# Writing out the loops over 208 gather groups in a four-layer graph network on one core

## The reference, cut to what matters

```
x = layernorm(x + attention_layer(x, src, dst, attr))        # stage e0
x = layernorm(x + sparse_mean_layer(x, src, dst))            # stage e1
x = layernorm(x + relational_layer(x, src, dst, edge_type))  # stages e2f and e2b
x = layernorm(x + transformer_layer(x, src, dst))            # two layers inside: e3a and e3b

# the common core of a stage
message = table[row_of_edge]                  # 103125 rows
out = segment_sum(weight * message, dst, num_segments=3125)
```

## Time and profile before

| | us |
|---|---|
| median of 3 runs | 9417.85 (9392.93 to 9419.25) |
| profiled execution, its own time | 9402.77 |
| its span, first to last instruction | 9401.0 |
| PE busy | 5084.4 (54%) |
| POOL busy | 5197.8 (55%) |
| DVE busy | 4670.5 (50%) |
| ACT busy | 1393.1 (15%) |
| mean granted TensorE clock | 0.719 of full speed |

### The profile page before, as it was taken

How to read it: one execution, slowest core, us unless ns; L and a number is a source line. 1 busy time by engine, 2 the same in 40 slices (tenths; PEclk the granted TensorE clock), 3 DMA queues, 4 the chain that set the end, 5 groups by cost and what they waited for, 6 DMA issues and landing times. The chain is left out here.

```text
span 9401.0 us, 104712 instructions
## 1 busy us (share of the span) xinstructions
PE 5084.4 (54%) x17609; PEld 3455.4 (37%) x17610; DVE 4670.5 (50%) x11390; ACT 1393.1 (15%) x5321; POOL 5197.8 (55%) x5325
## 2 busy tenths in 40 slices
PE   3444444455554139667766555555555555555555
PEld 2322222222222014344443333334444454555554
DVE  5565557555563214444444333335555555555555
ACT  3544442000000000000000000002111112111112
POOL 4555551555566740466665666664555554555553
PEclk7777767666666569888887666667777777777777
DMA  2222221222223014444444333332222222222222
GB/s 80 43 43 44 42 43 29 79 78 78 80 81 75 3 33 165 142 127 128 129 128 116 88 88 88 87 87 75 76 76 75 76 78 71 78 78 78 79 79 67
DMA packets 499181, 749.04 MB, mean 80 GB/s; under 512 B 217905, under 2 KB 351398, under 8 KB 498854
## 3 DMA queue, kind: packets, MB, share of 16 engines
q0 software_dynamic: 236352, 604.00, 23.3%
q1 hardware_dynamic: 262758, 144.28, 5.1%
HBM read 623.08 MB, written 124.79 MB: 80 GB/s over the span
## 5 line engine op out<-in xcount | busy, mean ns | idle before, releaser
L291 DVE TENSOR_TENSOR acc<-acc,ps 128x257 f32 (+3 forms) x4992 | 1883.2, 377 | 2418.8 <-issue 1127.2
L303 PE MATMUL ps<-rows,onehot 128*128 128x257 f32 (+1 forms) x4992 | 1879.5, 516 | 1646.3 <-DVE onehot L272 770.2
L263 POOL DMA_INDIRECT rows<-table,gidx x1664 | 1616.4, 971 | 1258.5 <-issue 510.8
L303 PEld LDWEIGHTS ps<-rows,onehot 128*128 128x128 f32 x4992 | 1113.4, 247 | 2471.8 <-issue 1404.6
L303 PE MATMUL ps<-msg,onehot 128*128 128x136 f32 (+1 forms) x4992 | 1295.2, 422 | 837.9 <-ACT msg L712 349.4
L303 PEld LDWEIGHTS ps<-msg,onehot 128*128 128x128 f32 x4992 | 1026.8, 266 | 1079.4 <-issue 890.9
L263 POOL DMA_INDIRECT rows<-table2f,gidx x832 | 796.9, 958 | 875.4 <-DMA table2f<-big 391.9
L263 POOL DMA_INDIRECT rows<-table3a,gidx x832 | 825.8, 993 | 616.6 <-ACT gidx L1202 343.8
L263 POOL DMA_INDIRECT rows<-table3b,gidx x832 | 823.0, 989 | 585.5 <-ACT gidx L1202 286.6
L263 POOL DMA_INDIRECT rows<-table2b,gidx x832 | 796.6, 958 | 473.6 <-issue 246.9
L1243 PE MATMUL ps<-big,msg 128*128 x3328 | 638.9, 353 | 511.8 <-issue 292.3
(11 more groups left out here) (309 smaller groups left out, 4601.1 us busy)
## 6 DMA issues: line engine op xcount, KB each, us to landing
table2f<-big SPq DMA_DIRECT2D x80, 640.0 KB, 4.6
table2b<-msg SPq DMA_DIRECT2D x200, 256.0 KB
rows<-table,gidx POOLq DMA_INDIRECT x1664
slots_d<-recs_d SPq DMA_DIRECT2D x832, 2.5 KB
rows<-table2f,gidx POOLq DMA_INDIRECT x832
rows<-table2b,gidx POOLq DMA_INDIRECT x832
rows<-table3a,gidx POOLq DMA_INDIRECT x832
rows<-table3b,gidx POOLq DMA_INDIRECT x832
```

What stands on the lines that cost most here:

```text
L263: nc.gpsimd.indirect_dma_start(out=rows[:, j, 0:width], out_offset=None, in_=table[:, :], in_offset=bass.IndirectOffsetOnAxis(ap=gidx[:, h ...
L291: nc.vector.tensor_tensor(acc[:, bass.ds(b * width, width)], acc[:, bass.ds(b * width, width)], ps[:, bank + k, 0:width], ALU.add).then_in ...
L303: nc.tensor.matmul(ps[:, bank + k, 0:width], onehot[:, h, k, :], rhs, start=True, stop=True).then_inc(sem(of(s, "tile_sum")), 1)
```

## The change

All loops over the groups become Python loops, so that each group has its own instructions on every engine and n is a number when the program is written. No transfer, no product, no vector operation and no order on an engine is changed. The block numbers remain data: DVE still loads them and works out the address from them, and so does PE for the queries. The loops over the blocks of the dense layers (`blocks`, `dense_act`), over the pairs of relations and over the 25 blocks in SP's `pb_store` stay as they are. A copy of e0, which the program skips if the exponents' range was right, is written out too.

```diff
         def groups(eng, body):
 
-            for n in range(R):
+            for n in range(NG):
                 body(n, n % R)
-            with eng.Fori(R, NG - 2 * R + 1, R) as n0:
-                for h in range(R):
-                    body(n0 + h, h)
-            for n in range(NG - R, NG):
-                body(n, n % R)
...
         def groups_beside(eng, body, unit):
 
             assert NG == PAIRS * (NB + 1)
-            for n in range(PAIRS):
-                body(n, n % R)
-            for j in range(PAIRS):
-                body(PAIRS + j, j % R)
-                unit(0, j)
-            with eng.Fori(2, NB + 1) as i:
+            for i in range(NB + 1):
                 for j in range(PAIRS):
                     body(i * PAIRS + j, j % R)
-                    unit(i - 1, j)
+                    if i > 0:
+                        unit(i - 1, j)
...
@@ att_groups
-            with eng.Fori(R, NG - 2 * R + 1, R) as n0:
+            for n0 in range(R, NG - R, R):
                 for h in range(R):
                     step(n0 + h, h, NG)
...
@@ e1 on DVE, the groups with the sort
-                with dve.Fori(0, SORT_IT) as i:
+                for i in range(SORT_IT):
...
@@ e1 on DVE, the last groups
-                with dve.Fori(rest, NG // R) as i:
+                for i in range(rest, NG // R):
...
@@ e1 on PE
-                    with eng.Fori(1, COUNTED // R) as i:
+                    for i in range(1, COUNTED // R):
...
-                    with eng.Fori(COUNTED // R + 2, NG // R) as i:
+                    for i in range(COUNTED // R + 2, NG // R):
```

## The result

The changed kernel takes 9125.39 us (median of 4 runs, 9112.79 to 9137.10) beside 9405.39 us for the kernel before (median of 4 runs, 9382.73 to 9419.25). The ratio is 0.9701, 95% interval 0.9682 to 0.9719: faster by 3.0%, 280 us. The forecast was 8780 us. The sign and the range held; the sum had 642 us where 280 came. One execution of the kernel before, beside the runs of series c further down, took 10685.17 us at a granted clock of 1.0 of full speed, and it is in no ratio of this text.

What follows compares the result with a forecast made beforehand. The prediction took engines waiting for each other as the bound, none busy over 55%. Terms 150 + 97 + 90 + 50 + 155 + 100 = 642 us off the 9401.0 us span gave 8780 us, range 8200 to 9440.

Steps and rivals of the forecast that it cites:

- The floor and the excess: Six gather stages: POOL's 0.95 + 0.30 us a gather stay, 5.00 us a group; the 1838 us above is all to win.
- The experiment in e1: Groups with DVE already written out in e1: excess over 5.00 us falls 43%, slow phase begins about 16 us in, not 7.
- (a): DVE's wait values and addresses become constants in e0, e1 and e2b: 150, 97 and 90 us less.
- rival 2: No change, 9418 us: gathers make the slow phase; e2b already runs at 6.01 us a group in a loop; chance 0.13.
- (b): PE is late in e2f, e3a and e3b; half the share, 21%, taken: 50 us and 155 us less.
- (c): The other four engines lose their register instructions too: 100 us less, a fifth of the 523 us upper bound.
- (d) to (f): Loop-end branches, POOL's one register instruction a group, SP's register work: all hidden, nothing gained.
- (g): Instruction loads for written-out code, about 227 on DVE: hidden in sequence, nothing taken, bounds 0 and 908 us.
- rival 3: Slower by the code: instruction loads meet the gathers and come late, 908 us lost against 642 gained, 9684 us; chance 0.17.
- The reading of "issue": DVE's wait called "issue" before L291 in e2b, 326.8 us in 1100 us, should fall by half or more.
- The sign of being wrong: If the slow phase still begins 7 us into a POOL run, register instructions had no part in it.
- Rival 1: Slow phase vanishes and stages go at POOL's pace: 7580 us for all six, otherwise 8100 to 8500; chance 0.15.

Runs made afterwards that it cites:

- series c: Both kernels unchanged, plus kernels with stage e0 alone left in loops or alone written out, on one chip; kernel before 9340.78 us.
- series a: Variants of both kernels on one chip; kernel before 7321.64 us, without the late phase, which is what fills the difference to 9339 to 9405 us.
- series d: One engine or the rest written out, SP waits added, constant block numbers, on one chip; kernel before 7321.20 us, no late phase.
- d1_dve: Kernel before with only DVE's group loops written out, late phase absent: 7311.78 us, ratio 0.9983.
- a3_sp_nops: Changed kernel plus 40 no-ops a group on SP in e2b, e3a and e3b, which did not become work; late phase absent: 7380.78 us, ratio 1.0079.
- e1_dve: Kernel before with only DVE's group loops written out, late phase present: 9216.83 us, ratio 0.9851.
- e2_rest: Kernel before with PE, ACT, POOL and SP written out and DVE in loops, late phase present: 9206.65 us, ratio 0.9852.
- c0_before: Kernel before, unchanged, run again for its profile with the late phase present: one run of 9343.33 us.
- c1_after: Changed kernel, unchanged, run again against the kernel before with the late phase present: 9007.97 us, ratio 0.9634.
- e4_const: Changed kernel with block numbers as constants, so sums go to other blocks, late phase present: 8844.04 us, ratio 0.9452 to the kernel before.
- d3_sp_waits: Changed kernel plus waits on an already high semaphore on SP in e2b, e3a and e3b, late phase absent: 7364.61 us, ratio 1.0055.
- d2_rest: Kernel before with PE, ACT, POOL and SP written out and DVE in loops, late phase absent: 7336.18 us, ratio 1.0019.
- c2_e0_loops: Changed kernel with e0 and its second pass left in loops on all engines, late phase present: 9098.42 us, ratio 0.9735 to the kernel before.
- series e: The four kernels of series d run again on a chip with the late phase; kernel before 9344.41 us.

## Why the prediction was wrong, step by step

- **The floor and the excess**: the 0.95 + 0.30 us stayed, and 5.00 us a group is reached: 5.04 in e2b of series a and d. The excess is real, but it belongs to the late phase and not to the kernel: of 1838 us only 114 us (d1_dve) to 178 us (a3_sp_nops) are left where that phase is absent, and the kernel before, at 7321 us, is there within 10 us of d1_dve's 7312.
- **The experiment in e1, (a)**: right where it was read. e1 was to win 97 us and won 89 and 112. The step from 7 to 16 us was read off two single runs of POOL's; in the mean it is from 11 to 15 us (13 to 16 in series c). e0 was given 150 us on DVE's account and won 113 and 87, but not on that account: in e1_dve it takes 1352.0 us, in e2_rest, on the same chip, 1324.6 and in c0_before 1338.7. Carrying the 43% to e2b failed: 90 us forecast, 24 and 24 measured; there the slow phase moves only from 7 to 10 us (8 to 10). e1_dve shows that DVE alone does in e1 what the stretch had promised (1247.8 against c0_before's 1339.0 us) and next to nothing in e2b (1230.2 against 1237.8), as rival 2's remark had warned: e2b ran at 6.01 us in its loop already.
- **(b), the step that failed most**: "I take half the share, 21%", 155 us for e3a and e3b, measured 10 us on the first chip and 74 on the second; and 50 us for e2f, 24 and 29 measured. The share was a guess with no row behind it (and no row showed e2f's waits), and what ends last in e3 is word from PE, which came later still. What happened in its place: the engines fill a run of e3 with 23 recorded instructions a us before the change and 21 after it, so the slow phase begins at 7 us in place of 6 and stays. By the instruction records of c0_before and c1_after, the change takes 17.6 register, semaphore and branch instructions a group out of e3a, 15.9 out of e2b and 15.5 out of e1; the gains come to 10, 7 and 35 ns for each. e4_const shows that e3 does pay for instructions: 119 us for another 4100, 29 ns each. Why the price differs so between stages is not settled.
- **(c)**, 100 us for the other engines on top of (a) and (b): as a mechanism right and underrated, e2_rest alone gives 138 us beside DVE's 128. As a term on top of (a) and (b) it failed: the stage gains, with these engines in them, are all there is, and it was (a) and (b) that put too much down to DVE. The shortfalls against 150, 97, 50, 90, 155 and 100 us are 37, 8, 26, 66, 145 and 100 us, 382 together, and 642 - 382 = 260 us is what the stages gave.
- **(d) to (f)** at nothing: no run speaks against it.
- **(g), the code**: right. 469 instruction packets against the "several hundred"; in series d the whole change written out has e2b at 1049.5 us, so the loads in sequence cost at most 9.5 us in that stage. The 908 us are excluded and rival 3 with them. The Trainium skill, Runtime: NRT & Kernel Launch, section Instruction fetch mechanics, has kernels prefer full unrolling where possible, since a taken branch to a target outside the two pages held costs a fetch stall. As far as fetches go the change could only win by it; no run here shows such a stall at a loop's end, and without the late phase the change costs 0.5 to 0.8%, for e0's gathers and not for a fetch.
- **The reading of "issue"**: expected down by half or more, and it went from 326.8 to 103.3 us; but I took it for the cost and it was only where the cost was booked. A sum over all of the line's late waits, "issue" with "remote", would have been the thing to forecast: it went from 445 to 500 us.
- **The sign of being wrong**, a slow phase that still begins 7 us into a run, is answered by stage: 11 to 15 us in e1, 7 to 10 in e2b, 6 to 7 in e3. The register instructions have a part in it, and in e3 a small one.
- **Rival 1**, that the slow phase vanishes, did not come: 1579 us of the excess stay.
- **Rival 2** had part of the truth: the late phase goes with POOL's runs. Its "no change" is out, with 0.970 and 0.963 where the phase is there.

**What stays open** is what the engines share. The traces show no resource that fills. Transfers are not slower: the DMA packets of e2b take 149 ns in the mean in d1_dve and 148 ns in e1_dve, one kernel at the two levels. The Trainium skill, NOTIFIC — the notification-queue block, section 7.1, says that the block which takes the engines' trace records holds its producers up rather than lose a record inside, and can so stall an engine; section 10 there puts what it holds at the order of 500 records, has a record cost the engine zero cycles, and gives a rate of at least 6.6 million a second as sustained without overflow. As an estimate from the earlier trace rows, one record an instruction would be 104712 in 9401 us, 11 million a second. A recorder that drains more slowly at some times than at others could give the dependence on the number of instructions of any engine, the beginning after a nearly constant number of them, and the two levels on one chip. No run here shows it, and two things don't fit a plain limit on records: d1_dve, where nothing is late, has 94991 instructions in 7314 us, 13 million a second, and in c1_after e2b goes at 6.3 and e3a at 11.5 recorded instructions a us. The same could come from another thing that is shared. Every execution of this text comes with a granted clock and a span, so all were recorded; no run shows whether one without recording has a late phase, or gains anything from the change.

## What to carry to other kernels

When instructions of several engines are late together, an engine's "issue" is no measure of what its own instructions cost: sum "issue" and "remote" before a line, and count the instructions of all engines up to the moment when things get late. A natural experiment in a trace holds for its own stage; carry its share to another only where that stage's waits look the same. Measure such a change more than once: the same change gave 0.970, 0.963 and, where the late phase was absent, 1.006 to 1.008 (in kernels that hold it). DVE alone written out is the choice that never lost more than 0.1% and gave 1.5%; the whole change is better with the late phase (3.0 to 3.7%) and worse without it. No version tried is shown to beat both under both; c2_e0_loops, which leaves e0 in loops, gave 2.7 and 2.8% with the late phase and was not run without it.

## What the runs showed of the hardware

- One kernel has two levels that lie 28% apart, 7321 and 9339 us, on one chip in two series. The mean granted clock is about 0.83 of full speed at the one and 0.72 at the other, but PE is no bound at either (5023 us busy in c0_before), POOL's gathers take 0.95 us at both, and the slow phase is there at a granted clock of 1.00 too; the difference is idle time.
- At the level of 9339 us the slow phase begins 5 to 17 us into a run of gathers, after 100 to 178 recorded instructions of all engines.
- There a recorded instruction less, of whatever engine, gave 11 to 16 ns of the whole kernel's time in the mean (table of series e), 7 to 35 ns by stage. For the bystander it is (28.5 + 32.8) us over some 5700 instructions, 11 ns, in e3, and nothing in e2b.
- An indirect gather that begins in the first 0.2 us of DVE's product over 128x512 takes 1.18 to 1.35 us in the mean (d1_dve, d3_sp_waits, d2_rest; 1.42 us in the one shown) and not 0.94 us; one that begins just before the product is not stretched.
